# Cross attention of a decoder layer: the pieces of the projections, of the packed operands and of the output gathered in the even steps of a written-out pipeline

## What is computed

```python
q = (x @ Wq).reshape(b, n, 32, 16)
k, v = jnp.split(ctx @ Wkv, 2, axis=-1)
q, k = apply_axial_rope(q, pos), apply_axial_rope(k, pos)
w = jax.nn.softmax(jnp.einsum('bqhd,bkhd->bhqk', q, k) * 16 ** -0.5, axis=-1)
attn = jnp.einsum('bhqk,bkhd->bqhd', w, v).reshape(b, n, 512)
out = x + attn @ Wout + bout
```

## Time and profile before

| | us |
|---|---|
| median of 3 runs (lowest, highest) | 1399.88 (1399.16, 1401.53) |
| span of the profiled execution | 1407.2 |
| retention, up to | 353.3 |
| cross attention | 353.3 to about 724 |
| feed-forward | from about 724 |
| busy in the whole span: PE | 1329.2 (94%) |
| DVE | 853.9 (61%) |
| POOL | 509.8 (36%) |
| ACT | 486.5 (35%) |

### The profile page before, as it was taken

The page is one execution under the profiler, slowest core; times in us unless marked ns, Lnnn a source line. Parts: engine busy times, 40 slices in busy tenths (PEclk is TensorE's granted clock), DMA queues, the critical chain, the costliest instruction groups (busy, mean ns, idle before and its releaser), DMA issues. The chain is left out here.

```text
span 1407.2 us, 24145 instructions
## 1 busy us (share of the span) xinstructions
PE 1329.2 (94%) x8442; PEld 1070.7 (76%) x8442; DVE 853.9 (61%) x1519; ACT 486.5 (35%) x764; POOL 509.8 (36%) x359
## 2 busy tenths in 40 slices
PE   7999999998899999999889999999999999999974
PEld 5777778776667777776567888888877899999963
DVE  6776666687888888887644665555561442222246
ACT  4222233243466666565754111111111233323310
POOL 1122222234543434432330038411160875563044
PEclk9999999999899999999999999999999999999997
DMA  7992000003664555447100014220001443542247
GB/s 259 325 327 84 0 0 0 0 16 120 182 176 140 168 162 161 148 140 206 28 23 0 24 66 151 97 80 23 23 23 49 182 141 139 185 164 82 73 138 239
DMA packets 85035, 159.83 MB, mean 114 GB/s; under 512 B 8576, under 2 KB 61952, under 8 KB 81536
## 3 DMA queue, kind: packets, MB, share of 16 engines
q1 hardware_dynamic: 78688, 124.19, 28.0%
q0 software_dynamic: 6272, 34.61, 7.0%
HBM read 109.22 MB, written 69.47 MB: 127 GB/s over the span
## 5 line engine op out<-in xcount | busy, mean ns | idle before, releaser
L1526 ACT ACTIVATE b_pf<-b_rt,b_zero 128x1024 f32<-128x1024 f32 x128 | 142.9, 1116 | 119.8 <-PE b_rt L1197 119.3
L1366 DVE TENSOR_REDUCE b_mx<-b_rt 128x4 f32<-128x1024 f32 x128 | 156.3, 1221 | 35.9 <-PE b_rt L1185 35.4
L2058 DVE SCALAR_TENSOR_TENSOR residual<-c_yp,c_shared,residual 128x512 f32<-128x512 f32 x144 | 103.8, 745 | 114.9 <-PE c_yp L43 110.5
L41 PE MATMUL c_fc<-c_xh,c_w 128*128 128x512 f32 x352 | 137.7, 391 | 0.0
L43 PE MATMUL c_fc<-c_xh,c_w 128*128 128x512 f32 x352 | 137.1, 389 | 0.0
L42 PE MATMUL c_fc<-c_xl,c_w 128*128 128x512 f32 x352 | 136.9, 389 | 0.0
L41 PE MATMUL c_fc<-c_ring,c_xTl 128*128 x312 | 105.6, 338 | 3.2 <-issue 3.2
L2196 ACT ACTIVATE c_s<-c_fc 128x512 f32<-128x512 f32 x44 | 26.3, 598 | 232.5 <-PE c_fc L43 226.9
L43 PE MATMUL c_fc<-c_ring,c_xTh 128*128 x312 | 101.3, 325 | 0.0
L42 PE MATMUL c_fc<-c_ring,c_xTh 128*128 x312 | 101.0, 324 | 0.0
L1878 POOL TENSOR_TENSOR c_w<-c_wraw,c_zero 128x1536 fp32r<-128x1536 f32 x9 | 24.8, 2750 | 202.5 <-DMA c_wraw<-in_c_ws 108.5
(11 more groups left out here) (402 smaller groups left out, 3498.5 us busy)
## 6 DMA issues: line engine op xcount, KB each, us to landing
weights_b<-b_pack SPq DMA_DIRECT2D x128, 200.0 KB
c_eraw<-in_c_we POOLq DMA_DIRECT2D x8, 2176.0 KB, 9.5
b_pack<-b_hi SPq DMA_DIRECT2D x56, 256.0 KB, 2.5
c_rows_in<-in_b_ctx SPq DMA_DIRECT2D x39, 256.0 KB, 9.8
c_rows_out<-in_b_ctx SPq DMA_DIRECT2D x39, 256.0 KB, 9.9
c_xe<-c_rows_in SPq DMA_DIRECT2D x39, 256.0 KB, 3.0
c_rows_out<-c_ye SPq DMA_DIRECT2D x39, 256.0 KB, 2.1
c_wraw<-in_c_ws SPq DMA_DIRECT2D x11, 768.0 KB, 4.2
```

The source lines that it names most:

```text
L41: nc.tensor.matmul(out, ll, rh, start=start, stop=False)
L1366: nc.vector.tensor_reduce(out=mx[:, :, 2 * p:2 * p + 2].rearrange("p t e -> p e t"), in_=rt[:, 0:2, :].rearrange("p e (t s) -> p e t s", s ...
L1526: nc.scalar.activation(pf[:, s:s + 2, :], rt[:, 2:4, :], ACT.Exp, scale=XD ** -0.5, bias=zero[:, :]).then_inc(e_done, 1)
L2058: nc.vector.scalar_tensor_tensor(out=X[:, t, :], in0=yp[:, (n * 4 + k) % 3, :], scalar=shared[:, t:t + 1], in1=X[:, t, :], op0=ALU.mult, o ...
```

## The change

The list of pieces is written anew, so that each entry holds all parts of a piece, at even steps only: w1 at 32, k0 and k1 at -14, x at -12, q0 at -10, q1 at -8, v0 and v1 at -6, o at 28, w0 at 30. Modulo 16 these are the steps 0, 2, 4, 6, 8, 10, 12 and 14. The list `ENDS` becomes `TAKES`, with the step of the take written in: one after the piece, two for k1. So takes stand in odd steps, k1's in step 4. `SUMS` follows. The transposes o of batch g - 1 now stand in the same step (12) as the first `group` of batch g, which writes the same tile attn; a wait for them is added ahead of that write.

```diff
         T, LAGS, LAGV = 16, 8, 11
-        PLAN = [(32, "w", 1, (0, 1)), (33, "w", 1, (2,)), (34, "w", 1, (3,)), (-14, "k", 0, (0,)), (-13, "k", 0, (1,)),
-                (-12, "x", 0, (0,)), (-12, "x", 1, (0,)), (-11, "k", 1, (0, 1)),
-                (-10, "q", 0, (0, 1)), (-9, "q", 0, (2,)), (-8, "q", 0, (3,)), (-8, "q", 1, (0,)), (-7, "q", 1, (1,)), (-6, "q", 1, (2, 3)),
-                (27, "o", 0, (0,)), (27, "o", 1, (0,)), (-4, "v", 0, (0, 1)), (-3, "v", 1, (0,)), (-2, "v", 1, (1,)),
-                (30, "w", 0, (0, 1)), (31, "w", 0, (2, 3))]
+        PLAN = [(32, "w", 1, (0, 1, 2, 3)), (-14, "k", 0, (0, 1)), (-14, "k", 1, (0, 1)), (-12, "x", 0, (0,)), (-12, "x", 1, (0,)),
+                (-10, "q", 0, (0, 1, 2, 3)), (-8, "q", 1, (0, 1, 2, 3)), (-6, "v", 0, (0, 1)), (-6, "v", 1, (0, 1)),
+                (28, "o", 0, (0,)), (28, "o", 1, (0,)), (30, "w", 0, (0, 1, 2, 3))]
...
-        ENDS = [use[:3] for use in PLAN if PARTS[use[1]] - 1 in use[3]]
+        TAKES = [(use[0] + (2 if use[1:3] == ("k", 1) else 1),) + use[1:3] for use in PLAN]
...
-        SUMS = (-12, -10, -7, -5)
+        SUMS = (-13, -12, -9, -7)
...
                 own.step(nc.vector.reciprocal(rs[:, :], src[:, :, XD]))
+                if q == 0 and not fresh(g):
+                    for t in range(TB):
+                        dve.wait_ge(gm_mm[BANK["o", t]], uses(g - 1, "o", t))
...
-                    for step, what, n in ENDS:
-                        for d in due(i, live, step + 1):
+                    for step, what, n in TAKES:
+                        for d in due(i, live, step):
...
```

## The result

The changed kernel takes 1436.61 us (median of 4 runs, 1435.28 to 1437.18) against 1399.72 us: 36.9 us more, ratio 1.0261 (1.0247 to 1.0275). Forecast were 1430.6 us, range 1417 to 1443, and slower with a chance of 0.93.

What follows compares the result with a forecast made beforehand. PE bounds the attention, with DVE close behind and tied to it once per step. First body 2.7, second 3.5, five steady batches of 4.9 and end 0 make 30.7 us, on 1399.9 gives 1430.6; range 1417 to 1443.

Steps and rivals of the forecast that it cites:

- The step table: Steps 0 to 15 of a steady attention batch, priced singly: 48.6 us together against 43.73, 4.9 more per batch.
- the second body: Second pass of the attention, without w1: 46.0 us against 42.45, +3.5.
- the end: Last two passes of the attention, with few blocks left: 0, between -2 and +2 us.
- steps 7 and 9: Odd steps with the takes of q0 and q1 ahead of the maximum: 2.6 us each, 0.8 more than PE needs.
- the first body: First pass of the attention, only step 2 partly at the lower clock: 41.7 us against 38.92, +2.7.
- the blocks of steps 6, 8 and 10: Steps with whole blocks q0, q1 and v in the attention's first pass: 3.4, 3.9 and 3.9 us.
- Fewer switches decide: Rival, attention: eight fewer switches per batch, 6 us less, 1394, if new waits stay below 0.9 us per batch; chance 0.05.
- Part of the wait is covered: Rival, steady batches: takes of x, o and k1 start earlier, a batch is 46.5 us, total 1419; chance 0.13.
- steps 4, 5 and 13: Steps where k1's take, x's subtractions and o's take with group 0 delay the maximum: 3.25, 2.9 and 3.1 us.
- The clock falls: Rival: PE's waits in steps 4 and 5 or 12 and 13 halve its clock once per batch: 12 us, 1443; chance 0.12.
- The bounds of 9 us each way: Uncertainty of the total: nine long odd or x steps off by 0.15 each, 1.4 per batch, 9 in all.

Runs made afterwards that it cites:

- experiments 3 and 5: The changed kernel with only q's takes one step later: 1440.62 us; and with the takes of q, x, o and w behind maximum and negation: 1434.71 us.
- Experiment 4: The changed kernel with five extra unused products in steps 1, 3, 5, 7 and 9 of the first body: 33.0 us above the kernel before.
- the plain swap: The changed kernel with the maximum ahead of all takes in DVE's step: 1469.1 us, ratio 1.0428 to the kernel before.

## Why the prediction held, and where it was off

The step table was right almost line by line: no step is off by more than 0.14 us. One steady batch, predicted and as measured from the rows of 495.56 to 543.59 us:

```
step       0    1    2    3    4    5    6    7    8    9    10   11   12   13   14   15   sum
predicted  4.10 2.20 3.87 2.00 3.25 2.90 3.87 2.60 4.10 2.60 3.87 1.83 2.26 3.10 3.87 2.20 48.6
measured   4.00 2.12 3.90 1.90 3.39 2.77 3.90 2.67 4.12 2.59 3.80 1.83 2.12 3.00 3.82 2.10 48.03
```

Five such batches give +23.0 us for 24.5 expected, although one of them carries 1.5 us of lower clock; the second body +3.4 for 3.5; the end +0.7 for 0. PE is busy for 87.5% of the steady part, for the 88% expected, and DVE for 37.2 us per batch, for 37. The mechanism, DVE's queue with the take ahead of the maximum, is what the waits show (5.4 us per batch), and experiments 3 and 5 take away the waits where they move the takes: steps 7 and 9 fall to 1.83 us in both. Whether some order of the queue would make the new list the better one stays open: each that I tried brought other waits.

The term that failed is the first body: "the others 2.0 + 3.25 + 2.9 + 3.4 + 2.6 + 3.9 + 2.6 + 3.7; together 41.7, +2.7". It was 49.24, +10.3. I let only step 2 run partly at the lower clock, as the old body does, and priced the blocks of steps 6, 8 and 10 at full clock; they took 5.38, 6.78 and 5.17 us. The prediction had the clock as a rival, but looked for it in the steady batches, where it came once in five, and not where PE has the least to do: in the first body the odd steps up to 9 have no products with v, and PE stood still for 1.3 to 2.2 us in each. Experiment 4 shows that it was that: with the gaps filled the body is 43.24 us, 1.5 from my figure. What is left of the excess is not in the blocks but near the body's end: step 13 took 2.98 us at a clock of 0.68, and 1.83 us without the extra products; why stays open.

The rivals. *Fewer switches decide* fell: the waits are 5.9 us per batch, 5.4 more than before, against the 0.9 at which it decides. PE's busy time per batch went from 43.14 to 42.0 us at full clock, 1.1 less, with the same products. I had put such a gain down to changes of shape, from the 0.34 us between the first product behind those with v and its successor. That reading doesn't carry it: the same 0.1 us stands behind transposes, which have the shape 128*128 of the block itself, 0.21 us where the width costs 0.119:

```profile
514.50 0.36 PE L41 MATMUL b_gm<-b_xh,weights_a 128*128 128x256 f32 x1
514.71 0.28 PE L42 MATMUL b_gm<-b_xl,weights_a 128*128 128x256 f32 x1
```

So the 1.1 us belong to eight fewer starts and ends of a block; whether to the change of shape in them, no run shows. The Trainium skill, TensorEngine Tiling (Array Packing), Key Properties, says that a change of tiling mode drains the TensorE; the sign of the trace agrees with it, and no row here separates it. The rough balance of a batch: -1.1 of PE's work, +5.4 of waits. *Part of the wait is covered* did not come: steps 4, 5 and 13 took 3.39, 2.77 and 3.00 us, close to the table's figures. *The clock falls* came in another place than I had put it, and cost more there than in the batches.

The bounds of 9 us each way were worked out from the long steps of the batches. That they held the miss of 7.6 us in the first body, for which no bound had been set, is luck, and so is part of the total's closeness: the steady part came out 1.5 us under my sum, and the attention began 0.85 us earlier.

## What to carry to other kernels

Where two engines exchange a buffer once per step, write down for each step what stands ahead of the releasing instruction in the other engine's queue, not only the sums of work: a list that is better for PE alone (1.1 us less per batch here) lost 5.4 us, because it put the other engine's longest work into the steps that hold least of PE's. Before moving such work behind the releasing instruction, list all who wait for that queue: the plain swap took away one group of waits and made several others, and the time rose. And price large blocks in a thinly filled stage at the lower clock too, above all the first pass of a pipeline, where half of the work of a steady step is still missing.

## What had not been expected of the hardware

In the first body of the changed kernel, blocks of 12 and 24 matmuls with gaps of 1.3 to 2.2 us before them ran for the greater part at 1.2 GHz (mean granted clock 0.51 to 0.67), while the steady batches, whose waits were 1.3 us at most, mostly stayed at 2.4 GHz. Adding 25 matmuls in the gaps made the stage 6 us shorter. In the kernel before a like filling raised the clock from 0.52 to 0.82 in its slow stretch and the time stayed, since PE then waited for DVE instead.
